# Batches of a feed-forward and an attention taken in another order, and a recurrence's first step laid between the steps of the attention's last batch

## What is computed

```python
def _L1_ffn_ref(x, ...):                       # two norms, 256 -> 1024 -> 256, token by token
    h = (x - mu) * rsqrt(var + EPS) * ln_gamma + ln_beta
    y = silu(h @ w1 + fc1_bias)
    return x + 0.5 * (y @ w2 + fc2_bias)

def _L2_xattn_ref(querys, keys, ...):          # one head, 64 context tokens, batch by batch
    weights = softmax(where(mask == 0, NEG, q @ k.T), axis=2)
    return weights @ v

def _L2_ffn_ref(x, ...):                       # a recurrence over the 8 batches
    def step(c, xt):
        ft = sigmoid(xt @ wf.T + c @ uf.T + bf)
        it = sigmoid(xt @ wi.T + c @ ui.T + bi)
        gt = tanh(xt @ wc.T + c @ uc.T + bc)
        return ft * c + it * gt, None
    c_final, _ = lax.scan(step, c0, x)         # scan over the batch axis, 0 to 7
    return tanh(einsum('tbi,oi->tbo', x, wo) + c_final @ uo.T + bo)
```

## Time and profile before

| | us |
|---|---|
| median of 3 runs | 2569.96 (2567.8 to 2570.36) |
| time of the profiled execution | 2567.9 |
| its span, first to last instruction | 2565.8 |
| PE busy | 2389.8 (93% of the span) |
| DVE busy | 1356.0 (53%) |
| ACT busy | 963.2 (38%) |
| PE on the chain that ended last | 82% |

### The profile page before, as it was taken

One profiled execution on the slowest core, in us unless ns is written; L12 is line 12 of the kernel. 1 busy time (PEld: TensorE's weight loads), 2 busy tenths in 40 slices (PEclk: granted clock), 3 DMA queues, 4 the chain that ended last, 5 costly groups with the idle time before them and its releaser, 6 DMA issues.

```text
span 2565.8 us, 38406 instructions
## 1 busy us (share of the span) xinstructions
PE 2389.8 (93%) x13932; PEld 1569.5 (61%) x13932; DVE 1356.0 (53%) x2952; ACT 963.2 (38%) x2238; POOL 593.3 (23%) x548
## 2 busy tenths in 40 slices
PE   7997999999999998988999889988985999999998
PEld 4444676766666665444666644544654777777776
DVE  7886654764445546885655333348884232233232
ACT  2366655454455543322333212234642222222221
POOL 3233221261010013102322000034454111111111
PEclk8998999999999999999999989989996999999999
DMA  5012101030010010100001089002126222222221
GB/s 196 1 34 90 39 9 50 25 104 29 26 50 25 26 38 13 69 1 17 1 1 35 1 280 308 0 0 107 59 74 250 34 34 34 34 32 32 34 34 25
DMA packets 73757, 144.54 MB, mean 56 GB/s; under 512 B 11592, under 2 KB 62537, under 8 KB 71121
## 3 DMA queue, kind: packets, MB, share of 16 engines
q1 hardware_dynamic: 41280, 100.94, 11.6%
q0 software_dynamic: 16368, 26.23, 5.3%
q10 hardware_dynamic: 15936, 15.03, 2.1%
HBM read 107.42 MB, written 71.09 MB: 70 GB/s over the span
## 4 chain that ended last, share of the span: by engine, by line
PE 82%; DVE 9%; ACT 4%; issue 2%; POOL 1%; DMA 1%; SPq 0%; DVEq 0%; POOLq 0%; ACTq 0%
PE PS L2278 13%; PE PS L2300 7%; PE PS L2697 4%; PE PS L1534 4%; PE PS L1525 4%; PE PS L2709 4%; PE PS L2003 3%; PE PS L2014 3%; PE PS L599 3%; PE PS L2766 3%; PE PS L2757 3%; PE PS L2731 3%; PE PS L2802 2%; PE PS L674 2%; DVE mem L1140 2%; DVE mem L1145 2%
## 5 line engine op out<-in xcount | busy, mean ns | idle before, releaser
L2278 PE MATMUL PS<-mem,ctx2T 128*128 x1136 | 350.0, 461 | 4.0 <-SPq L2242 3.2
L2278 PEld LDWEIGHTS PS<-mem,ctx2T 128*128 128x128 f32 x1136 | 211.4, 191 | 110.8 <-issue 6.3
L2460 POOL DMA_INDIRECT out_x<-xnT,moe_small x71 | 110.1, 1551 | 481.9 <-ACT xnT L2355 481.9
L2424 DVE TENSOR_TENSOR ctx2T<-PS,ctx2T 128x352 f32<-128x352 f32 x142 | 74.5, 525 | 246.3 <-PE PS L2278 246.3
L2300 PE MATMUL PS<-mem,moe_small 128*128 x852 | 195.7, 379 | 1.1 <-DVE moe_small L2432 1.1
L2300 PEld LDWEIGHTS PS<-mem,moe_small 128*128 128x128 f32 x852 | 156.4, 190 | 19.9 <-issue 1.4
L1145 DVE RECIPROCAL mem<-PS 128x512 f32<-128x512 f32 x48 | 160.9, 3352 | 12.4 <-PE PS L668 12.3
L2429 DVE COPY moe_small<-PS 128x512 f32<-128x512 f32 x71 | 49.1, 692 | 173.1 <-PE PS L2288 173.1
L1140 DVE TENSOR_REDUCE mem<-PS 128x32 f32<-128x2048 f32 x48 | 109.9, 2290 | 51.6 <-PE PS L624 51.4
L3082 DVE TENSOR_REDUCE moe_small<-PS 128x2 f32<-128x1024 f32 x64 | 78.4, 1226 | 101.9 <-PE PS L2757 101.9
L3227 POOL TENSOR_TENSOR mem<-mem,moe_small 128x512 f32<-128x512 f32 x64 | 82.2, 1304 | 211.6 <-DVE moe_small L3092 211.6
(11 more groups left out here) (373 smaller groups left out, 4601.2 us busy)
## 6 DMA issues: line engine op xcount, KB each, us to landing
slots<-in_trash_rows SPq DMA_DIRECT2D x8, 4290.0 KB, 63.2
mem<-in_L_ffn_experts SPq DMA_DIRECT2D x8, 2176.0 KB, 14.0
xn<-unit_rows SPq DMA_DIRECT2D x15, 512.0 KB, 4.0
xn<-slots ACTq DMA_DIRECT2D x53, 130.0 KB, 2.1
x_all<-in_x SPq DMA_DIRECT2D x8, 512.0 KB, 8.4
mem<-unit_rows SPq DMA_DIRECT2D x8, 512.0 KB, 3.9
out_x<-x_all ACTq DMA_DIRECT2D x8, 512.0 KB, 3.4
unit_rows<-moe_small SPq DMA_DIRECT2D x7, 512.0 KB, 3.2
```

The source lines that it names most:

```text
L2278: last = nc.tensor.matmul(PS[:, 1 + 2 * g + half, 0:HE], m.rowT[:, j % 2, k, :], w[:, :, at:at + HE], start=k == 0, stop=k == KD - 1)
L2460: nc.gpsimd.indirect_dma_start(s.T["out"], bass.IndirectOffsetOnAxis(s.token[:, j % 4:j % 4 + 1], 0), m.result[:, j % 4, :], None, compute ...
```

## The change

The batches of L1_ffn and L2_xattn come as 7, 0, 1, ... 6 (`OF_SLOT`) where they came as 7, 6, ... 0. So batches 0 and 1 of `x` are ready long before the last attention, which now is that of batch 6. Batch 0 is normed and transposed for the recurrence in the last turn of L1_ffn. The recurrence's turn 0 is taken out of the loop, cut into pieces, and the pieces are written between the steps of the last attention on every engine; gate i, whose banks 4 and 5 the attention uses, comes behind it, with the norm and the transposes of batch 1. The last attention's product goes to banks 4 and 5 where it went to 0 and 1. The attention's rows get a transposed buffer of their own (`rowsT`), so that `xnT` is free for the recurrence. The loop keeps turns 1 to 7. The recurrence's semaphores are its own, and its stage start is gone (`entered`).

```diff
+OF_SLOT = (B - 1,) + tuple(range(B - 1))
...
@@ ffn1_pe
         if i + 1 < B:
             ffn1_front_pe(pe, e, s, i + 1)
+        else:
+            e.pe_transpose_xn(pe, x.next, 0)
         down(i, 3)
@@ ffn1_act
         if i + 1 < B:
             front(i + 1)
+        else:
+            e.act_copy_xnT(act, x.next, 0)
@@ ffn1_first_norm
-    dve.wait_ge(e.x_updated, s.x_before - NT + TB * (i + 1))
+    dve.wait_ge(e.x_updated, s.x_before - (NT - TB if i == 0 else 0))
     for t in range(TB):
-        order.mark(dve.bn_stats(e.stats[:, t, :], e.x_all[:, (B - 1 - i) * TB + t, :]))
+        order.mark(dve.bn_stats(e.stats[:, t, :], e.x_all[:, OF_SLOT[i] * TB + t, :]))
@@ ffn1_dve
+        else:
+            ffn2_variance(dve, order, e, x.next, 0)
...
+        else:
+            dve.wait_ge(s.sems["residual"], 2 * B)
+            e.ln_apply(dve, x.next, 0)
@@ ffn1_pool
+        else:
+            e.pool_rstd(pool, x.next, 0)
@@ plan_xattn2
-    s.kT = take(KD, B * SC)
+    s.kT = s.rowsT = take(KD, B * SC)
 def xattn2_last_pe(pe, e, s):
-    xattn2_turn_rows(pe, e, s, B - 1)
-    xattn2_scores(pe, e, s, B - 1)
-    xattn2_turn_probs(pe, e, s, B - 1)
-    xattn2_out(pe, e, s, B - 1)
+    f, j = s.next, B - 1
+    pe.wait_ge(f.weights_loaded, 16 * len(f.loads))
+    pe.wait_ge(f.xnT_ready, KD)
+    ffn2_gate_of_rows(pe, e, f, 0)
+    pe.wait_ge(s.previous.sems["added"], NT)
+    ffn2_gate_of_rows(pe, e, f, 2)
+    xattn2_turn_rows(pe, e, s, j)
+    pe.wait_ge(f.sems["c_ready"], 1)
+    ffn2_gate_of_state(pe, e, f, 0)
+    xattn2_scores(pe, e, s, j)
+    ffn2_gate_of_state(pe, e, f, 2)
+    ffn2_own(pe, e, f, 0)
+    ffn2_own(pe, e, f, 1)
+    xattn2_turn_probs(pe, e, s, j)
+    ffn2_own(pe, e, f, 2)
+    xattn2_out(pe, e, s, j, bank=4)
+    ffn2_own(pe, e, f, 3)
+    pe.wait_ge(e.x_updated, f.x_before)
+    ffn2_gate_of_rows(pe, e, f, 1)
+    pe.wait_ge(f.sems["own_ready"], TB)
+    e.pe_transpose_xn(pe, f, 1)
+    ffn2_gate_of_state(pe, e, f, 1)
 
 def xattn2_last_act(act, order, e, s):
-    xattn2_copy_rows(act, e, s, B - 1)
-    xattn2_exponentials(act, e, s, B - 1)
-    xattn2_copy_probs(act, e, s, B - 1)
+    f, j = s.next, B - 1
+    xattn2_copy_rows(act, e, s, j)
+    act.wait_ge(f.weights_loaded, 16 * len(f.loads))
+    xattn2_exponentials(act, e, s, j)
+    xattn2_copy_probs(act, e, s, j)
+    for n, g in enumerate((0, 2, 1)):
+        if g == 1:
+            e.act_copy_xnT(act, f, 1)
+        for m in range(KD):
+            act.wait_ge(f.sems["gate_psum"], KD * n + m + 1)
+            ffn2_gate(e, f, g, m)
 
 def xattn2_last_dve(dve, order, e, s):
-    xattn2_norm(dve, order, e, s, B - 1)
-    xattn2_rows(dve, e, s, B - 1)
-    xattn2_shift(dve, order, e, s, B - 1)
-    xattn2_sums(dve, order, e, s, B - 1)
-    xattn2_add(dve, e, s, B - 1)
+    f, j = s.next, B - 1
+    dve.wait_ge(f.weights_loaded, 16 * len(f.loads))
+    xattn2_norm(dve, order, e, s, j)
+    dve.tensor_copy(f.cT, f.c0.rearrange("p (k o) -> p k o", o=1).broadcast_to([P, KD, S])).then_inc(f.sems["c_ready"], 1)
+    xattn2_rows(dve, e, s, j)
+    ffn2_variance(dve, order, e, f, 1)
+    xattn2_shift(dve, order, e, s, j)
+    e.ln_apply(dve, f, 1)
+    xattn2_sums(dve, order, e, s, j)
+    ffn2_own_rows(dve, e, f, 0, 0)
+    ffn2_own_rows(dve, e, f, 0, 1)
+    xattn2_add(dve, e, s, j, bank=4)
+    ffn2_own_rows(dve, e, f, 0, 2)
+    ffn2_own_rows(dve, e, f, 0, 3)
+    ffn2_state(dve, order, e, f, 0)
 
 def xattn2_last_pool(pool, order, e, s):
     xattn2_power(pool, e, s, B - 1)
+    e.pool_rstd(pool, s.next, 1)
@@ plan_ffn2
+    s.entered = s.previous
@@ new helpers, cut out of the loop of ffn2_pe and ffn2_dve
+def ffn2_gate_of_rows(pe, e, s, g):
+    for m in range(KD):
+        for k in range(KD):
+            e.nc.tensor.matmul(e.PS[:, 2 + KD * g + m, :], s.wx[g][:, k, m * P:(m + 1) * P], e.xnT[:, k, :],
+                               start=k == 0, stop=False)
...
+def ffn2_own(pe, e, s, t):
...
 def ffn2_pe(pe, e, s):
     PS, nc = e.PS, e.nc
-    pe.wait_ge(s.weights_loaded, 16 * len(s.loads))
     NG = 3 * KD
-    e.pe_transpose_xn(pe, s, 0)
-    pe.wait_ge(s.sems["c_ready"], 1)
-    with pe.Fori(0, B) as i:
+    with pe.Fori(1, B) as i:
         pe.wait_ge(s.xnT_ready, KD * (i + 1))
+        pe.wait_ge(s.sems["gate_ready"], NG * i)
         for g in range(3):
...
+def ffn2_state(dve, order, e, s, i):
...
+    with dve.Fori(1, B) as i:
```

More of the change, by code:

```diff
@@ L144, in mark, with turn @@
         self.k += 1
[L146 to L147 removed]
+    def turn(self, i, per, first=0):
+        self.base, self.i, self.per, self.k = self.base + self.k - first * per, i, per, 0
     def end(self, turns):
@@ L1988, in plan_ffn2, with ffn2_gate_of_state @@
     s.pe, s.act, s.dve, s.pool = ffn2_pe, ffn2_act, ffn2_dve, ffn2_pool
+def ffn2_gate_of_rows(pe, e, s, g):
[3 more added lines that the diff above has]
+                               start=k == 0, stop=False)
+def ffn2_gate_of_state(pe, e, s, g):
+    for m in range(KD):
+        for k in range(KD):
+            last = e.nc.tensor.matmul(e.PS[:, 2 + KD * g + m, :], s.wc[g][:, k, m * P:(m + 1) * P], s.cT[:, k, :],
+                                      start=False, stop=k == KD - 1)
+        last.then_inc(s.sems["gate_psum"], 1)
@@ L1991, in ffn2_pe @@
+def ffn2_own(pe, e, s, t):
+    for k in range(KD):
+        last = e.nc.tensor.matmul(e.PS[:, t // 2, (t % 2) * D:(t % 2 + 1) * D], e.xnT[:, k, t * P:(t + 1) * P],
+                                  s.wo[:, k, :], start=k == 0, stop=k == KD - 1)
+    last.then_inc(s.sems["own_psum"], 1)
 def ffn2_pe(pe, e, s):
     PS, nc = e.PS, e.nc
-    pe.wait_ge(s.weights_loaded, 16 * len(s.loads))
     NG = 3 * KD
-    e.pe_transpose_xn(pe, s, 0)
-    pe.wait_ge(s.sems["c_ready"], 1)
-    with pe.Fori(0, B) as i:
+    with pe.Fori(1, B) as i:
@@ L1998, in ffn2_pe @@
         pe.wait_ge(s.xnT_ready, KD * (i + 1))
+        pe.wait_ge(s.sems["gate_ready"], NG * i)
         for g in range(3):
[L2000 to L2004, removed]
+            ffn2_gate_of_rows(pe, e, s, g)
         for t in range(TB):
-            for k in range(KD):
-                last = nc.tensor.matmul(PS[:, t // 2, (t % 2) * D:(t % 2 + 1) * D], e.xnT[:, k, t * P:(t + 1) * P],
-                                        s.wo[:, k, :], start=k == 0, stop=k == KD - 1)
@@ L2009, in ffn2_pe @@
-            last.then_inc(s.sems["own_psum"], 1)
+            ffn2_own(pe, e, s, t)
         pe.wait_ge(s.sems["c_ready"], i + 1)
         for g in range(3):
[L2012 to L2016, removed]
+            ffn2_gate_of_state(pe, e, s, g)
@@ L2025, in ffn2_pe, with ffn2_gate @@
     last.then_inc(s.sems["last_psum"], 1)
+def ffn2_gate(e, s, g, m):
+    e.nc.scalar.activation(s.gates[:, g, m, :], e.PS[:, 2 + KD * g + m, :], ACT.Tanh if g == 2 else ACT.Sigmoid,
+                           bias=s.bg[:, g, m:m + 1]).then_inc(s.sems["gate_ready"], 1)
 def ffn2_act(act, order, e, s):
-    PS, nc = e.PS, e.nc
-    act.wait_ge(s.weights_loaded, 16 * len(s.loads))
-    e.act_copy_xnT(act, s, 0)
     NG = 3 * KD
-    with act.Fori(0, B) as i:
+    with act.Fori(1, B) as i:
         act.wait_ge(s.sems["c_ready"], i + 1)
@@ L2037, in ffn2_act @@
                 act.wait_ge(s.sems["gate_psum"], NG * i + KD * g + m + 1)
-                nc.scalar.activation(s.gates[:, g, m, :], PS[:, 2 + KD * g + m, :], ACT.Tanh if g == 2 else ACT.Sigmoid,
-                                     bias=s.bg[:, g, m:m + 1]).then_inc(s.sems["gate_ready"], 1)
+                ffn2_gate(e, s, g, m)
             if g == 1:
@@ L2079, in tail_add, with ffn2_variance @@
     dve.scalar_tensor_tensor(tiles, f.own[:, b * TB:(b + 1) * TB, :], f.gate, tiles, ALU.mult, ALU.add).then_inc(e.x_updated, TB)
-def ffn2_dve(dve, order, e, s):
-    PS = e.PS
-    dve.wait_ge(s.weights_loaded, 16 * len(s.loads))
-    NG = 3 * KD
-    dve.tensor_copy(s.cT, s.c0.rearrange("p (k o) -> p k o", o=1).broadcast_to([P, KD, S])).then_inc(s.sems["c_ready"], 1)
-    e.dve_layernorm(dve, order, s, 0)
-    with dve.Fori(0, B) as i:
-        order.turn(i, e.LN_MARKS + 2)
+def ffn2_variance(dve, order, e, s, i):
+    for t in range(TB):
+        e.ln_stats(dve, order, i, t)
+    e.ln_variance(dve, order, s)
@@ L2090, in ffn2_dve @@
+def ffn2_dve(dve, order, e, s):
+    with dve.Fori(1, B) as i:
+        order.turn(i, e.LN_MARKS + 2, first=1)
         for t in range(TB):
-            dve.wait_ge(s.sems["own_psum"], TB * i + 2 * (t // 2) + 2)
-            dve.tensor_tensor(s.own[:, i * TB + t, :], PS[:, t // 2, (t % 2) * D:(t % 2 + 1) * D], s.bo, ALU.add)\
-                .then_inc(s.sems["own_ready"], 1)
+            ffn2_own_rows(dve, e, s, i, t)
         e.dve_layernorm(dve, order, s, i + 1)
-        dve.wait_ge(s.sems["gate_ready"], NG * i + 2 * KD)
```

64 lines of the change are left out of this document (37 added, 27 removed).

## The result

The changed kernel takes 2543.68 us (median of 4 runs, 2540.55 to 2545.05), the kernel before 2570.16 us beside it: 26.5 us less, a ratio of 0.9901 with a 95% interval of 0.9889 to 0.9913. The prediction was 2546.0 us.

A forecast was written before the change was run, and what follows sets the result against it. PE bounds the kernel, so only its idle or low-clock time can go: 0.87 + 31.16 + 0.1 = 32.1 us replaces 56.05, 24.0 off the median 2569.96, giving 2546.0 us; range 2543 to 2550.5.

The forecast's parts named there:

- The bound: Whole kernel: PE, busy 93% of the span, bounds it; only its idle or lower-clock time can be had.
- The order by itself: L1_ffn and L2_xattn: the new order of the batches alone costs nothing and brings nothing.
- PE's layout: Behind L1_ffn's last `down`: PE's pieces laid end to end at full-clock durations, reaching +31.16 us.
- nine such switches: PE's new stretch, upper bound: each switch between small groups costs 0.2 us, 1.6 more in all, 22.4 off.
- What must be ready: New stretch: DVE's and ACT's parts are done before PE asks, such as attention's rows at +5.1 against +6.9.
- The slack of the probabilities: Last attention: shift and exponentials done at +15.7, PE asks for the probabilities at +18.1; 2.4 us of slack.
- The sum: From the last `down` to the loop's first turn: 32.1 us in place of 56.05, so 24.0 us off.
- The clock's part: Last attention and first turn's products: at least 7.6 of the 24.0 us are half clock, the rest mostly waiting.
- The late attention: Last attention: 4.2 us of DVE's extra work between its steps all lies on the chain; 2550.2 us, 9%.
- The case of 2548.2: Up to the loop: one fetch waits behind one packet of the table's transfers, 2.2 us; 4%.
- The low clock: New stretch: PE at clock 0.50 throughout, its 31 us of work taking 31 more; 2577 us, 2%.
- given back: Behind the stretch: table transfers end 3 us later while L3_xattn comes 24 us earlier, losing the gain; 2570 us, 3%.

The follow-up runs named there:

- the order alone: The kernel before with the batches of L1_ffn and L2_xattn in the order 7, 0 to 6 and nothing else of the change; ratio 1.0000.
- the four additions of 5.00 us: The changed kernel with four 128x1024 additions on DVE between the last attention's scores and its shift; stretch 34.90 us, one run.
- 11 products added: The kernel before with 11 products of 128x512 that nothing reads, added where PE idles in the last attention; ratio 0.9981, stretch 51.01 us.

## Why the prediction was right

**The bound.** PE with its idle time and its clock was what the stretch hung on; no other engine took over.

**The order by itself, nothing.** Right: 1.0000 with 0.0009 either way.

**PE's layout.** Predicted and measured behind the last `down`: transposes of the attention done at +7.77 and +7.74, scores at +12.95 and +12.91, probabilities at +18.57 and +18.56, values at +21.35 and +21.35, batch 1's transposes at +26.97 and +26.96, loop at +31.16 and +31.17. The two surcharges that I took from rows, 0.2 behind the values and 0.25 behind a wait, are there (1.06 for 0.87; 3.68 for 3.45), and no other above 0.05: the upper bound of nine such switches was far off.

**What must be ready.** All of it was, one part later than laid out. The attention's rows are there at +5.5 and not at +5.1, with PE asking at +6.9: the copy of the start state was to fall into DVE's wait for POOL's power and cost nothing, but beside it POOL takes 1.38 us for that power, in every profile with the copy there, and 1.01 in every one without. It ate slack only.

```profile
1464.15 1.38 POOL L1906 TENSOR_TENSOR mem<-mem,minus_half 128x4 f32<-128x4 f32 x1 [30.42 <-DVE mem L1898]
```

The slack of the probabilities, predicted at 2.4, is 2.4 in the profile and by experiment, where 2.5 us cost 0.33 and 5.0 cost 2.86. The adds have 1.61, not 1.4. The 0.1 for the wait ahead of gate i was not needed.

**The sum.** 24.0 us in the stretch (unrounded, 56.05 - 32.13 = 23.9), measured as 24.01. The 32.04 was forecast to 0.1 us and repeats; that the difference agrees as closely is in part luck, as the 56.05 is good to about 1 us only. The medians differ by 26.5 and 24.6; the extra is within the interval; in the first pair of profiles it lies outside the stretch, where the work is the same.

**The clock's part.** Here the prediction misread a row. It put 7.6 or more on the clock from four rows; one of them, 1.26 for the attention's transposes, is mostly DVE's pace, and 0.39 of it the clock, so that the four come to 6.7. The measured part, at least 7.1 (6.2), holds more than those four rows, batch 0's transposes and those of the probabilities too. The total didn't hang on this split. Nor was the clock's 1.00 after 4.2 us without work, in the forecast a point against a low clock, much of a point: it fell to 0.50 at 1468.2, 1.2 us after PE had resumed, and with the order alone it fell inside the same wait: PE idled from 1465.15 to 1469.30, and the window 1468 to 1469 has 0.73 and the next one 0.50, so it fell at about 1468.5, some 3.3 us into the wait. In the new stretch no wait is longer than 0.8 us, PE is at full work on both sides of it, and the clock stayed at 1.00.

```profile
1467.00:1468.00 1.00, 1.00 (x4) 0.44 (x4) 0.91 (x3) 0.00 (x0) 0.00 (x0) 1.00 0.00 0
1468.00:1469.00 1.00, 1.00 (x5) 0.71 (x5) 0.00 (x0) 0.60 (x1) 0.00 (x0) 0.60 0.00 0
```

(Windows of the kernel before, in which PE resumes at 1466.99.)

**The rivals.** The late attention needed more than 2.4 us of lateness and has none. That DVE does things in the written order is seen with the four additions of 5.00 us: the shift starts behind them, at 1485.37, with the scores done at 1480.3. The case of 2548.2 adds 2.2 us for a fetch of instructions that waits behind one packet; no run shows such a fetch. The chain of the changed kernel shows PE's pieces end to end from 1457.09 to 1491.83 and, at the entry of the loop, 0.02 us of issue, ACT's 0.70 and 0.04 more, as at its second turn. The low clock did not come: it is 1.00 throughout. That the 31 us of work would take 31 us more at 0.50 was the author's estimate; the pieces that it can rest on are the scores, 3.66 us for 1.73, and the values, 3.79 for 1.92, and with 11 products added the scores took 3.52 at 0.50. The gain was not given back: from the loop's first turn to the end there are 1047.9 us, where from the second turn before there were 1046.9. L3_xattn took 266.4 us against 265.6, by the forecast's own list a sign against it; but on the second chip it took 264.6 and 265.1 in two profiles with the change and 265.9 in one without it, so the 0.8 is within what executions differ by.

## What to carry to other kernels

Where a block whose steps wait for each other stands alone at the end of a stage, look for work of the next stage that needs none of its results, and choose the order of the tiles so that such work exists; then lay it between the steps, longest piece where the other engine needs longest. Sum the busy engine's pieces from rows at the clock that it will have, and check every other engine's part against the time at which it is asked for: the slack found so was right to 0.5 us here. Then look at what the wait at the top of a loop protects: here it cost 1.05 us a turn for banks that the first products don't touch.

## What the runs showed of the hardware

The longest wait doesn't tell what the granted clock will be. In the run with 11 added products it fell from 1.00 to 0.50 at 1472.8 us, where PE had waited twice, for 0.74 and 0.84 us, with eight transposes between that took 1.74 for 0.87 us of work. In the one with DVE 5.0 us late it stayed at 1.00 through a wait of 2.67 us with PE at full work on both sides. And ahead of the recurrence's last products the same wait of 3.71 us was followed by a fall to 0.50 in one profile of the changed kernel and by none in the other. Where all waits of the last attention were filled to under 0.5 us the clock stayed at 1.00 for the whole stretch.

Stretches with unchanged work differ between executions: the time up to L1_ffn's last product by up to 8 us, and L3_xattn took 264.6 to 283.3 us. Much of the second goes with the chip: 273.8 to 283.3 in six profiles from one, 264.6 to 265.9 in three from another, where the kernel before is 11 us faster too. So kernels are compared on one chip. What in the chip does it was not looked for. A stretch that is all PE's work at a granted clock of 1.00 repeats to 0.01 us (32.04 twice, 31.27 and 31.26) and is the better measure of a change of this size than the total; one with the clock at 0.50 in it (56.05 and 55.12) does not.
